# A histogram on the matrix engine in a graph and attention kernel: products of two edge columns on one side of the array for half of the blocks

## The reference

```python
src = jnp.concatenate([edge_index[0], loops])
dst = jnp.concatenate([edge_index[1], loops])
e = jax.nn.leaky_relu(a_src[src] + a_dst[dst], negative_slope=0.2)
...
agg = jax.ops.segment_sum(msg, dst, num_segments=M).reshape(M, HEADS * NUM_EXPERTS) + b_gat
```

## Time and profile before

| | |
|---|---|
| median of 3 runs | 908.27 us (906.5 to 909.39) |
| the profiled execution, its own time | 905.63 us |
| its span (first to last instruction) | 903.9 us |
| busy: PE, DVE, ACT, POOL | 609.3, 741.0, 311.7, 326.3 us |
| TensorE clock granted, mean | 0.821 of full |

### The profile page before, as it was taken

One profiled execution on the slowest core, in us unless ns is written; L12 is line 12 of the kernel. 1 busy time (PEld: TensorE's weight loads), 2 busy tenths in 40 slices (PEclk: granted clock), 3 DMA queues, 4 the chain that ended last, 5 costly groups with the idle time before them and its releaser, 6 DMA issues.

```text
span 903.9 us, 12612 instructions
## 1 busy us (share of the span) xinstructions
PE 609.3 (67%) x4608; PEld 304.0 (34%) x4608; DVE 741.0 (82%) x1500; ACT 311.7 (34%) x469; POOL 326.3 (36%) x384
## 2 busy tenths in 40 slices
PE   1602564259788888888877788589979888722620
PEld 1200122013334444444342344444434443422620
DVE  3699989397868888888878785799999999869466
ACT  1650461023445555555534353421211111111006
POOL 2000100005657777777100000077777777700000
PEclk9956675555979999999977899699999999965755
DMA  6000103200000000000000002141101111100001
GB/s 183 0 1 0 50 16 84 55 1 1 1 1 1 2 1 0 0 0 0 0 1 1 1 1 94 24 91 11 11 9 11 11 11 10 10 3 0 5 1 46
DMA packets 21990, 16.90 MB, mean 19 GB/s; under 512 B 13488, under 2 KB 18944, under 8 KB 21168
## 3 DMA queue, kind: packets, MB, share of 16 engines
q1 hardware_dynamic: 15424, 14.02, 5.6%
q0 software_dynamic: 5392, 2.18, 3.0%
q10 hardware_dynamic: 1120, 0.00, 0.1%
HBM read 10.51 MB, written 2.54 MB: 14 GB/s over the span
## 4 chain that ended last, share of the span: by engine, by line
DVE 50%; PE 31%; ACT 4%; issue 3%; SPq 2%; DMA 0%; DVEq 0%; POOL 0%; ACTq 0%; POOLq 0%
DVE arena L1392 12%; DVE mx L1312 11%; PE psum L607 9%; PE psum L755 4%; PE psum L662 3%; PE psum L623 3%; DVE arena L1394 3%; SPq L402 2%; DVE arena L1050 2%; PE psum L638 2%; DVE arena L1046 2%; ACT arena L1022 2%; PE psum L737 1%; PE psum L814 1%; DVE mz L1331 1%
## 5 line engine op out<-in xcount | busy, mean ns | idle before, releaser
L1312 DVE TENSOR_REDUCE mx<-psum 128x2 f32<-128x512 f32 x256 | 164.2, 683 | 60.7 <-PE psum L623 59.5
L492 POOL DMA_INDIRECT work<-node_rows,idx x160 | 158.1, 988 | 53.2 <-issue 48.5
L931 ACT ACTIVATE arena<-psum 128x1024 f32<-128x1024 f32 x128 | 131.0, 1024 | 113.4 <-PE psum L638 113.4
L607 PE MATMUL psum<-arena 128*32 128x256 f32 x1024 | 150.8, 420 | 1.0 <-ACT arena L936 0.5
L1392 DVE TENSOR_TENSOR arena<-arena,psum 128x4096 bf16<-128x4096 bf16 x64 | 146.0, 2281 | 3.8 <-PE psum L755 3.5
L755 PE MATMUL psum<-arena 128*128 128x512 bf16 x512 | 126.1, 392 | 26.1 <-DVE arena L1394 26.0
L469 POOL TENSOR_SCALAR work<-arena,cF 128x184 f32<-128x184 f32 x128 | 93.7, 743 | 113.7 <-DVE gone L1236 57.1
L623 PE MATMUL psum<-arena 32*128 32x256 bf16 x512 | 82.6, 301 | 31.9 <-DVE mx L1312 19.9
L755 PEld LDWEIGHTS psum<-arena 128*128 128x128 bf16 x512 | 46.8, 100 | 93.1 <-DVE arena L1394 41.9
L607 PEld LDWEIGHTS psum<-arena 128*32 128x32 f32 x1024 | 51.9, 116 | 62.8 <-issue 35.0
L471 POOL TENSOR_TENSOR work<-work,arena 128x368 f32<-128x368 f32 x64 | 61.9, 967 | 5.4
(11 more groups left out here) (302 smaller groups left out, 905.4 us busy)
## 6 DMA issues: line engine op xcount, KB each, us to landing
work<-work SPq DMA_DIRECT2D x48, 64.0 KB, 2.0
work<-node_rows,idx POOLq DMA_INDIRECT x160, 2.7
arena<-in_L_ffn_edge_index_dram SPq DMA_DIRECT2D x2, 1024.0 KB, 13.0
work<-edge_nodes SPq DMA_DIRECT2D x4, 368.0 KB, 6.3
digits<-arena SPq DMA_DIRECT2D x1, 1024.0 KB, 3.9
arena<-digits SPq DMA_DIRECT2D x1, 1024.0 KB, 6.0
arena<-in_jpat_dram SPq DMA_DIRECT2D x1, 1024.0 KB, 7.8
out_dram<-work SPq DMA_DIRECT2D x4, 256.0 KB, 2.3
```

Source lines behind the costliest of these rows:

```text
L492: pool.indirect_dma_start(gath[:, l, :], None, tab, bass.IndirectOffsetOnAxis(ap=idx[:, l:l + 1], axis=0)).then_inc(done, 16)
L607: mm = pe.matmul(ps[32 * j:32 * j + 32, 6, (g % 2) * 256:(g % 2 + 1) * 256], vstage[:, buf, kt, 4 * g + j, :], pbuf[:, m % 4, jj, kt, :], ...
L931: act.activation(pbuf[:, n % 4, :, :, :], ps[:, 2 + 2 * (n % 2):4 + 2 * (n % 2), :].rearrange("p j (k q) -> p j k q", k=U), ACT.Exp).then_ ...
L1312: v.reduce_max(mx[:, h, :], ps[:, h % 2, :].rearrange("p (u k) -> p u k", u=U), AX.X).then_inc(mx_done, 1)
```

## The change

The low one-hots are laid out in runs of q = 2 columns in place of 4, in all 64 blocks: the same number of elements, but of each row of `jp` only two elements are read before the next row. For blocks 0 to 31 and the last one the products keep their size: two neighbouring groups `k` of 64 weights are taken together as 128 weights, against the same 512 columns. For blocks 32 to 62 a product takes two columns: 64 weights by 256 columns, and 16 products a block in place of 8. Products alternate between the partitions 0 to 63 and 64 to 127 of the accumulator, and between the two halves of its column groups. `own_column` and `fold` follow the new layout, with one more small instruction on VectorE.

```diff
--- before.py
+++ after.py
@@ -207,11 +207,12 @@
         st_den = sb("st_den", [P, PER, 4])
         hbt = ft_hbt = part2(13312, 768).rearrange("p (b u f) -> p b u f", b=B, u=U)
         oh = part2(0, (HB + LB) * HC, BF16).rearrange("p (n j c) -> p n j c", n=2, j=HB + LB)
-        ohl = oh[:, :, HB:HB + LB, :].rearrange("p n j c -> p n (j c)").rearrange("p n (k m q) -> p n k m q", m=LB, q=4)
+        ohl = oh[:, :, HB:HB + LB, :].rearrange("p n j c -> p n (j c)").rearrange("p n (k m q) -> p n k m q", m=LB, q=2)
         jp = part2(8192, 2048, BF16).rearrange("p (j c) -> p j c", j=HB)
         hid = part2(10240, 2048).rearrange("p (n c) -> p n c", n=4)
         cnt = part2(12416, HB)
         own_column, cross = part2(12544 + CH, 4), part2(0, CH).rearrange("p (j q) -> p j q", q=4)
+        halves = part2(13200, 2 * LB).rearrange("p (h m) -> p h m", h=2)
         pdig = psum[:, 6, :].bitcast(BF16).rearrange("p (s c) -> p s c", s=2)
         pdig_w = psum[:, 6, :].rearrange("p (s c) -> p s c", s=2)
         dlt = work[0:LT, 0, 0:2 * P]
@@ -751,9 +752,16 @@
             def count(blk, buf, first, last):
 
                 pe.wait_ge(h_ready, blk + 1)
-                for c in range(0, HC, 4):
-                    mm = pe.matmul(ps[:, 7, :], ohl[:, buf, c // 4, :, :].rearrange("p m q -> p (m q)"), oh[:, buf, 0:HB, c:c + 4],
-                                   start=first and c == 0, stop=last and c == HC - 4)
+                if blk < NBLK // 2 or last:
+                    for k in range(0, HC // 2, 2):
+                        mm = pe.matmul(ps[:, 7, :], ohl[:, buf, k:k + 2, :, :].rearrange("p k m q -> p (k m q)"), oh[:, buf, 0:HB, 2 * k:2 * k + 4],
+                                       start=first and k == 0, stop=last and k == HC // 2 - 2)
+                else:
+                    for k in range(HC // 2):
+                        n = k % 2
+                        mm = pe.matmul(ps[64 * n:64 * n + 64, 7, :].rearrange("p (j q) -> p j q", q=4)[:, :, 2 * n:2 * n + 2],
+                                       ohl[:, buf, k, :, :].rearrange("p m q -> p (m q)"), oh[:, buf, 0:HB, 2 * k:2 * k + 2],
+                                       start=False, stop=False)
                 mm.then_inc(h_used, 1)
 
             def chunk(i, first, last):
@@ -1391,8 +1399,8 @@
                 here = slice(blk % 16 * HC, blk % 16 * HC + HC)
                 v.tensor_tensor(oh[:, buf, 0:HB, :], jp, pdig[:, 0, here].rearrange("p (j c) -> p j c", j=1).broadcast_to([P, HB, HC]),
                                 ALU.is_equal).then_inc(oneh, 1)
-                v.tensor_tensor(ohl[:, buf], jp[:, 0:LB, 0:4].rearrange("p (k m) q -> p k m q", k=1).broadcast_to([P, HC // 4, LB, 4]),
-                                pdig[:, 1, here].rearrange("p (k m q) -> p k m q", m=1, q=4).broadcast_to([P, HC // 4, LB, 4]),
+                v.tensor_tensor(ohl[:, buf], jp[:, 0:LB, 0:2].rearrange("p (k m) q -> p k m q", k=1).broadcast_to([P, HC // 2, LB, 2]),
+                                pdig[:, 1, here].rearrange("p (k m q) -> p k m q", m=1, q=2).broadcast_to([P, HC // 2, LB, 2]),
                                 ALU.is_equal).then_inc(h_ready, 1)
 
             def chunk(i):
@@ -1403,8 +1411,9 @@
                         list_one_hots_by_bucket()
                     one_hot_block(i * 16 + m, m % 2)
 
-            v.reduce_sum(fold[:], ident.rearrange("p (m q) -> p m q", m=LB), AX.X).then_inc(fold_ready, 1)
-            g.link(v.reduce_sum(own_column, ident.rearrange("p (m q) -> p q m", m=LB), AX.X))
+            g.step(v.reduce_sum(halves, ident.rearrange("p (h m q) -> p h m q", h=2, m=LB), AX.X))
+            g.link(v.reduce_sum(own_column.rearrange("p (h q) -> p h q", h=2), ident.rearrange("p (h m q) -> p h q m", h=2, m=LB), AX.X))
+            v.tensor_tensor(fold[:], halves[:, 0], halves[:, 1], ALU.add).then_inc(fold_ready, 1)
             v.wait_ge(jp_loaded, 16)
             v.wait_ge(hl_loaded, 16)
             v.wait_ge(lists_copied, 2)
```

## The result

The changed kernel takes 924.92 us, the median of 4 runs (924.27 to 926.48), against 908.0 (906.5 to 909.39, 4 runs): a ratio of 1.0189, 95% interval 1.0168 to 1.021. It is slower by 17 us. The forecast was 928, range 917 to 941. The profiled execution of the changed kernel took 926.48 us, the slowest of its four, with a span of 924.9.

The account below looks back on a forecast made before the run. VectorE's one-hots were taken to bound the histogram, narrowly ahead of TensorE. The profiled 905.63 us + 21.8 (low one-hots) - 2 (waits) = 925.4; with 2.6 us to the median, 928 us, range 917 to 941.

Parts of the forecast that it names:

- The low one-hots: VectorE, 64 histogram blocks: 512 moves at 0.66 ns add 0.34 us a block, +21.8 us, bounds 0 and +57.
- Rival 1: Low one-hots on VectorE: a move at every word costs nothing in bf16; 906.8 us, chance 0.10.
- rival 2: Low one-hots fall to one element at a time or pay more per move: 941 to about 963 us; chance 0.10.
- The second source in PSUM: Low one-hots' digits, the same PSUM word read 32 times: full rate, so no cost.
- The waits for TensorE: VectorE's 3.5 us of histogram waits for counts: 2 us go, bounds -3.5 and +2.
- The half-size products: TensorE, blocks 32 to 62: 0.9 us a block against 1.74, the upper bound; gains only part of the waits.
- Rival 4: Half-size products: the array's two sides do not work at once; 1.74 us a block, 928 us; inside the forecast's 0.72.
- rival 3: Histogram: TensorE's clock stays down, TensorE becomes the bound; mild form some 3 us a chunk, 934, inside the forecast's 0.72.
- dear form: Low TensorE clock in the histogram without overlap of the array's sides: +28 us twice, 984 us; chance 0.03.
- The last term: Whole kernel: the profiled execution lay 2.6 us under the median of the runs, so 925.4 was written as 928.

Follow-up runs that it names:

- the run with 2048 moves: Version with both one-hots grouped by two columns and all blocks half-size, its high one-hots reading 64-byte pattern rows instead of a packed table: 988.48 us.
- the packed pattern: Changed kernel with the 32 by 2 pattern values read by the low one-hots copied once to lie side by side: 907.96 us, ratio 1.0004.

## Why the prediction was right

**The low one-hots** were nearly the whole of it, as forecast. The size, 0.66 ns a move taken from a float32 write with the same 64 bytes, measured 0.64 in bf16 reads: 20.9 us in place of 21.8. Rival 1 (no cost in bf16) is refuted by 1006 ns, rival 2 (one element at a time) by the same number, which lies under 1226 and fits 512 moves; the run with 2048 moves gave the same price.

**The second source in PSUM**, costed at nothing from L1067, cost nothing: with the packed pattern the instruction takes 678 ns.

**The waits for TensorE**: 2 us forecast to go, 1.5 went. One sentence under this step is wrong: TensorE was not late only with its clock down. The kernel before has waits of 0.18 us before the high one-hots at 642.25, 692.95 and 742.03, and of 0.24 at 766.93, each with a granted clock of 1.00 over the 4 us before. Only 0.87 and 0.62 of its 3.5 us come right behind a low clock (0.57).

**The half-size products**: here the step failed, though nothing hung on it. I took 0.9 us a block by the overlap seen in L607 and gave 1.74 as the upper bound. It was the upper bound, but not for the reason that bound stood for. The sides overlap as L607's do; each reads at half the rate. Rival 4, that the two sides do not work at once, is wrong, and gave the right number. L607's products read 256 columns in order, and I carried its factor over to products that read runs of two. I had put the doubt on the output's runs, which cost nothing that the runs could show. The input's runs I had not weighed for TensorE at all, though I had just priced such reads for VectorE.

**The clock** (rival 3): no dear form appeared. In the changed kernel the clock of the second half fell a little, from 0.98 to 0.91 (the figure behind POOL):

```profile
699.00:807.50 108.50, 89.56 (x680) 50.89 (x676) 104.46 (x68) 16.07 (x33) 73.99 (x77) 0.91 0.13 10
```

In the version with all blocks half-size it was 0.82 to 0.84, and 3.7 us of waits stayed. The rival's 3 us a chunk do not come from its own sums, which differ by 1.2.

**The last term**, the 2.6 us by which the profiled execution lay under the median, was not borne out. The medians moved by 16.9 us, less than the 19.8 of the sum and less than the 18.7 of the two profiled stretches; without the term the forecast would have been 925.4. To carry the whole difference over assumes that a median execution waits in the histogram as little as the profiled one. It need not: the run with pairs 8 bytes apart has one-hots as fast as before and waited 7.3 us before its high ones in place of 3.8, of which 3.25 at one place at a granted clock of 0.50. Such waits a slower VectorE takes away. Whether that is it is not shown, since no median execution of the kernel before was profiled. Of the 3 us between 928 and 924.92, 0.9 are size, less 0.5 of waits, 0.7 the overlap and what is not placed, and the rest this term and scatter: the four runs span 2.2 us. The sum was too large by these 3 us, and the range held them.

## What to carry to other kernels

When a layout is changed to feed one engine, price the reads and writes of every engine that touches it: here words 16 or 64 bytes apart cost 0.64 to 0.75 ns each on VectorE, with the element count unchanged. A small table packed once takes such a cost away, since it is the pattern and not the data that is read far apart; its copy took 0.18 us here, ahead of a copy of digits that still sat idle 1.17 us for ScalarE. And do not count on a smaller product being faster: 16 half-size ones took as long as 8 full ones until their moving operand lay in order.

## What the runs showed of the hardware

VectorE lost its rate when successive words lay 16 or 64 bytes apart (0.75 and 0.64 ns a word) and not when they lay 8 bytes apart (678 ns, as in order). The table of the Trainium skill cited in the prediction ("Vector Engine (DVE) Microarchitecture Reference", section 5.2) asks for adjacent words; the run with 8 bytes, 678 ns, speaks against that wording. Another page of the Trainium skill, "SBUF — State Buffer" (section "Specifications (TRN2)"), asks for two or more hits in a line of 16 bytes, and with that both runs agree, 678 ns at 8 bytes and 1064 at 16. The changed kernel's own setup shows it once more in float32: `own_column` is summed over elements 8 bytes apart in 275 ns (L1415), and over elements 16 bytes apart in 371 before (L1407).

TensorE halved its rate with moving bf16 columns in runs of two, 64 bytes apart, and kept it with runs of four: 16 products of 256 columns in 1.90 us against 1.06 in order, 8 of 512 columns in 1.90. Writes to PSUM in runs of two float32 cost nothing that could be seen: 1.90 us with and without, and 1.06 with and without where the reads were in order.
